# A mixture of experts on sorted rows with a register-chosen expert, in a two-layer decoder kernel

## The reference, cut to what matters

```python
xc = layernorm(x).astype(bfloat16)
normed = (xc * rsqrt(mean(xc * xc) + EPS) * norm_weight).astype(bfloat16)
logits = normed @ gate_weight.T + gate_bias            # 8 experts
scores, idx = top_k(logits, 2)
w = softmax(scores)
combine = sum(one_hot(idx, 8) * w[..., None], axis=-2)
p1 = einsum('bsh,eoh->bseo', normed, mlp1_weight) + mlp1_bias
g, lin = minimum(p1[..., 0::2], 7.0), clip(p1[..., 1::2], -7.0, 7.0)
act = g * sigmoid(1.702 * g) * (lin + 1.0)
p2 = einsum('bsei,ehi->bseh', act, mlp2_weight) + mlp2_bias
x = x + xc + einsum('bseh,bse->bsh', p2, combine).astype(bfloat16)
```

## Time and profile before

| | |
|---|---|
| median of 3 runs | 2125.4 us (2123.68 to 2129.94) |
| profiled execution | 2127.73 us, its span 2125.9 us |
| TensorE busy | 1959.0 us, 92% |
| VectorE busy | 1382.6 us, 65% |
| ScalarE busy | 1030.1 us, 48% |
| GpSimd busy | 972.0 us, 46% |
| granted TensorE clock, mean | 0.967 of full speed |
| DMA | 95.80 MB, mean 45 GB/s |
| 960 KB strips of the bias table | 16 DMAs, 6.6 us to landing (page, DMA issues) |

### The profile page before, as it was taken

How to read it: one execution, slowest core, us unless ns; L and a number is a source line. 1 busy time by engine, 2 the same in 40 slices (tenths; PEclk the granted TensorE clock), 3 DMA queues, 4 the chain that set the end, 5 groups by cost and what they waited for, 6 DMA issues and landing times.

```text
span 2125.9 us, 53677 instructions
## 1 busy us (share of the span) xinstructions
PE 1959.0 (92%) x22085; PEld 1631.0 (77%) x22085; DVE 1382.6 (65%) x3093; ACT 1030.1 (48%) x2080; POOL 972.0 (46%) x762
## 2 busy tenths in 40 slices
PE   7999999999999999857787689999999999989994
PEld 5677777777777777546676579999999999988883
DVE  6667676767676766558777675555566455456983
ACT  3666666666666665514444444333245234334551
POOL 1555555555555555524444342443433343344441
PEclk9999999999999999979999889999999999999996
DMA  7001020101010101041230120000121000030000
GB/s 256 30 18 48 19 75 18 49 21 51 16 56 11 48 11 41 13 149 40 70 110 11 50 85 8 18 12 13 48 76 52 24 25 18 17 126 26 11 16 16
DMA packets 58787, 95.80 MB, mean 45 GB/s; under 512 B 6520, under 2 KB 51328, under 8 KB 56192
## 3 DMA queue, kind: packets, MB, share of 16 engines
q1 hardware_dynamic: 55696, 84.33, 12.1%
q10 hardware_dynamic: 2848, 8.04, 1.0%
HBM read 69.93 MB, written 22.41 MB: 43 GB/s over the span
## 4 chain that ended last, share of the span: by engine, by line
PE 41%; DVE 6%; issue 4%; POOL 3%; ACT 2%; DMA 1%; SPq 0%; POOLq 0%; DVEq 0%; ACTq 0%
PE psum L262 13%; PE psum L273 9%; PE psum L1936 4%; PE psum L1924 2%; PE psum L1299 2%; PE psum L1312 2%; PE psum L1910 2%; PE psum L2428 2%; PE psum L243 2%; POOL b_act_lo L1443 1%; DVE b_act L1509 1%; PE psum L222 1%; PE psum L2462 1%; ACT e_pr L2567 1%; DMA b_wvals_in<-wvals 1%
## 5 line engine op out<-in xcount | busy, mean ns | idle before, releaser
L811 POOL TENSOR_TENSOR a_sm<-a_sm,a_rsum 128x1024 f32<-128x1024 f32 x256 | 480.2, 1895 | 384.3 <-DVE a_rsum L845 381.9
L833 DVE CUSTOM_DVE_ANT_0 a_sm<-psum,a_strip 128x1024 f32<-128x1024 f32 x256 | 312.1, 1220 | 145.7 <-PE psum L667 145.6
L748 ACT ACTIVATE a_sm<-a_sm,a_mn 128x1024 f32<-128x1024 f32 x256 | 293.9, 1148 | 27.4 <-DVE a_mn L833 26.2
L753 ACT ACTIVATE a_pT<-psum 128x512 f32<-128x512 f32 x256 | 151.6, 592 | 274.7 <-PE psum L680 274.7
L680 PE MATMUL psum<-ident,a_sm 128*128 128x128 f32 x2048 | 275.8, 277 | 5.7 <-POOL a_sm L811 4.5
L680 PEld LDWEIGHTS psum<-ident,a_sm 128*128 128x128 f32 x2048 | 224.4, 141 | 63.2 <-issue 46.3
L695 PE MATMUL psum<-a_pT,a_V 128*64 128x256 f32 x2048 | 249.0, 385 | 0.6 <-ACT a_o L759 0.6
L695 PEld LDWEIGHTS psum<-a_pT,a_V 128*64 128x64 f32 x2048 | 136.1, 136 | 77.3 <-issue 22.1
L840 DVE COPY a_pT<-psum 128x512 f32<-128x512 f32 x256 | 175.0, 684 | 13.3 <-PE psum L680 6.0
L2020 ACT ACTIVATE g_val<-psum 128x512 f32<-128x512 f32 x64 | 38.2, 598 | 216.7 <-PE psum L1936 216.7
L1443 POOL TENSOR_TENSOR b_act_lo<-b_act,b_act_hi 128x512 fp32r<-128x512 f32 x64 | 90.4, 1417 | 107.9 <-ACT b_act_hi L1350 107.9
(11 more groups left out here) (344 smaller groups left out, 4183.9 us busy)
## 6 DMA issues: line engine op xcount, KB each, us to landing
a_strip<-table SPq DMA_DIRECT2D x16, 960.0 KB, 6.6
oT<-a_o SPq DMA_DIRECT2D x64, 128.0 KB, 1.8
b_oT_in<-oT SPq DMA_DIRECT2D x8, 1024.0 KB, 5.4
a_raw<-in_a_wqkv SPq DMA_DIRECT2D x7, 384.0 KB, 3.3
s_x<-in_x_rev SPq DMA_DIRECT2D x4, 512.0 KB, 7.3
b_x_in<-in_x SPq DMA_DIRECT2D x8, 256.0 KB, 5.7
b_w<-in_m_w ACTq DMA_DIRECT2D x1, 2048.0 KB, 10.3
x<-b_x SPq DMA_DIRECT2D x8, 256.0 KB, 2.2
```

The costliest lines, as they stand in the source:

```text
L748: a.activation(sm[:, st % RING, :], sm[:, st % RING, :], ACT.Exp, scale=-1.0, bias=mn[:, at:at + 1], accum_out=rsum[:, at:at + 1]).then_in ...
L753: a.activation(probs(st, 0), psum[:, 4, :].rearrange("p (k q) -> p k q", k=4), ACT.Copy).then_inc(sig("pT_act"), 1)
L811: g.tensor_tensor(sm[:, st % RING, :], sm[:, st % RING, :], rsum[:, at:at + 1].broadcast_to([P, T]), ALU.mult).then_inc(sig("scaled"), 1)
L833: v.tensor_tensor_reduce(out=sm[:, st % RING, :], in0=scores_banks(hl).rearrange("p c n -> p (c n)"), in1=strip[:, pair % 2, hl, qt * P:qt ...
```

## The change

`cross_and_mixture` is written anew in four parts, with the same attention and expert arithmetic.

1. Rounds r = 0 to 9 instead of steps: tile r in the front of cross attention, tile r - 1 in its end and the mixture's norm, tile r - 2 in gating. Here there are no experts. Per tile the two best experts are found with max and max_index; a count of earlier rows of each expert (products of `mask` with a triangle `below` and with ones, stage `mr`) gives every row its rank. GpSimd writes each tile's normed bf16 rows with four indirect DMAs (128 rows each, for each of two experts and two tiles of 128) to `xs` in DRAM: expert e has its rows from e x 2048 on. `xs` is filled with zeros before, in self-attention, by 9 DMAs on SyncE's queue.
2. Tables: from the counts VectorE makes, for each of 23 units, its expert (`owner_i`) and first row (`first_i`); 23 = (4096 - 8) // 256 + 8 is enough for any counts. It also gathers the biases of the unit's expert, and computes for every row where its result will lie (`found_at`).
3. 23 units of 256 rows: SyncE reads the first row into a register and loads the rows, TensorE reads the expert into a register, turns the rows (`xt`, copied by ScalarE), and multiplies with w1, pick and w2 addressed by that register. The arithmetic between is that of before, with rings of 3 buffers. The bias b2 is added by two products in `down`, VectorE copies the result (`results`) and SyncE stores it to `y` in DRAM.
4. When all is stored, GpSimd gathers with four indirect DMAs per tile the two result rows of each row, and VectorE weights and adds them (`combined`). The next stage's columns, queries and keys follow all units on TensorE; its norm and key copies stand between the combinations on VectorE.

The copies of w2 and pick move from VectorE to ScalarE. Cut to its core (removed lines of the old orders are left out):

```diff
+ROUTED = E0 * N + (E0 - 1) * CP
+FILLS = -(-ROUTED // P // FILL)
...
+                    if NG // 2 <= g < NG // 2 + FILLS:
+                        i = g - NG // 2
+                        sp.wait_ge(early["have"]("fill"), 1)
+                        rows = slice(i * FILL, min((i + 1) * FILL, ROUTED // P))
+                        part = S["xs"].rearrange("(p n) d -> p n d", p=P)[:, rows, :].rearrange("p n d -> p (n d)")
+                        sp.dma_start(part, early["zeros"][:, 0:part.shape[1]]).then_inc(early["have"]("fill"), 16)
...
+        def fetch_sorted(j):
+            at_row = sp.value_load(first_i[0:1, j:j + 1], min_val=0, max_val=ROUTED - CP)
+            if j >= UR:
+                sp.wait_ge(sig("xt_ps"), j - UR + 1)
+            sp.dma_start(xs[:, j % UR, :, :], S["xs"][bass.ds(at_row, CP), :].rearrange("(t p) d -> p t d", p=P)
+                         ).then_inc(sig(f"lx{j % UR}"), 16)
...
+        sp.wait_ge(sig("tables"), 1)
+        sp.wait_ge(routed("sc"), 16 * 2 * PT * NP)
+        for j in range(UR):
+            fetch_sorted(j)
+        then["load_projections"](sp)
+        for j in range(NU):
+            if j + UR < NU:
+                fetch_sorted(j + UR)
+            store_sorted(j)
...
+    def order(r):
+        a, b, c = r, r - 1, r - 2
+        every = [("ay", a + 1), ("mT", c), ("mg", c), ("bT", a), ("bp", b), ("by", b), ("bs", a), ("mr", c), ("ay_rest", a + 1)]
+        if r == 0:
+            every = [("ay", 1), ("ay_rest", 1), ("br", 0)]
+        if r == NP + 1:
+            every.append(("mc", 0))
+        return [(stage, s) for stage, s in every if 0 <= s < NP and not (s == 0 and stage in ("bT", "bp", "bs"))]
...
+        def turned(j):
+            pe.wait_ge(sig(f"lx{j % UR}"), 16 * (j // UR + 1))
+            part_columns(pe, sig, banks, "xt", j, xs[:, j % UR, :, :], identb, dt=BF16)
...
+                        last = pe.matmul(out, w1[:, k, bass.ds(e, 1), col:col + P].rearrange("p e n -> p (e n)"), xT[:, j % UR, k, :],
+                                         start=k == 0, stop=half == 0 and k == KC - 1)
+                    if half:
+                        last = pe.matmul(out, b1r[:, :], pick[:, bass.ds(e * KC + m, 1), :].rearrange("p e n -> p (e n)"),
+                                         start=False, stop=True)
...
+                pe.matmul(out, pick[:, bass.ds(e * KC, 1), t * P:(t + 1) * P].rearrange("p e n -> p (e n)"), b2r[:, :],
+                          start=True, stop=False)
...
+                                     w2[:, bass.ds(e, 1), k, :].rearrange("p e n -> p (e n)"),
...
+        for i in every_unit:
+            if i + ahead + 1 < NU:
+                expert[i + ahead + 1] = pe.value_load(owner_i[0:1, i + ahead + 1:i + ahead + 2], min_val=0, max_val=E0 - 1)
+                turned(i + ahead + 1)
+            if 0 <= i + ahead < NU:
+                up(i + ahead)
+            if i >= 0:
+                down(i)
...
+        for n in ["columns"] + [f"q{u}" for u in range(4)] + [f"k{u}" for u in range(4)]:
+            then["first_units"](pe, n)
...
-                                    ACT.Gelu_apprx_sigmoid, bias=b1[:, e, m:m + 1])
+                last = a.activation(gs[:, j % UR, m, :], banks("ug", j)[:, m * CP:(m + 1) * CP],
+                                    ACT.Gelu_apprx_sigmoid, bias=b1s[:, m, j:j + 1])
...
+        for i in every_unit:
+            if 0 <= i + 1 < NU:
+                high(i + 1)
+            if i + ahead + 1 < NU:
+                turned(i + ahead + 1)
+            if 0 <= i + ahead < NU:
+                gated(i + ahead)
...
+        def scatter(s):
+            g.wait_ge(sig("m_spot"), s + 1)
+            g.wait_ge(have("fill"), 1 + 16 * FILLS)
+            if s:
+                g.wait_ge(routed("sc"), 16 * 2 * PT * s)
+            for slot in range(2):
+                for t in range(PT):
+                    i = slot * PT + t
+                    g.indirect_dma_start(S["xs"][:, :], bass.IndirectOffsetOnAxis(rows_at[:, s, i:i + 1], 0),
+                                         nr[:, s % 3, t, :], None).then_inc(routed("sc"), 16)
...
+        def gather(s):
+            r = s % 2
+            if s >= 2:
+                g.wait_ge(sig("m_out"), s - 1)
+            for slot in range(2):
+                for t in range(PT):
+                    i = slot * PT + t
+                    g.indirect_dma_start(yg[:, r, slot, t, :], None, S["y"][:, :],
+                                         bass.IndirectOffsetOnAxis(found_at[:, s, i:i + 1], 0)).then_inc(routed(f"gy{r}"), 16)
...
+        for r in range(1, NP + 2):
+            s, b, c = r, r - 1, r - 2
+            if s < NP:
                 norm_rstd(g, sig, "bn", s, bn, mhalf)
...
+            if 0 < b < NP:
+                g.wait_ge(sig("b_inv"), b + 1)
                 g.tensor_tensor(pr[:, :, :], pr[:, :, :], spread(mx[:, :], WK), ALU.mult).then_inc(sig("b_probs"), 1)
...
+            if c >= 1:
+                scatter(c - 1)
             if s + 1 < NP:
                 first_sum(s + 1)
-            if back:
...
+        scatter(NP - 1)
+        for j in range(NU):
+            low(j)
+        for r in range(UR):
+            g.wait_ge(sig(f"sy{r}"), 16 * len(range(r, NU, UR)))
+        g.wait_ge(sig("tables"), 2 + KC)
+        for s in range(NP):
+            gather(s)
+            if s == 3:
+                then["first_root"](g)
...
+        for r in range(1, NP + 2):
+            s, b, c = r, r - 1, r - 2
+            if 0 < b < NP:
+                shifted(b)
             if s < NP:
...
+                joined(s)
+            if c >= 0:
+                normed(c)
+            if 0 < b < NP:
+                inverse(b)
+            if s < NP:
+                v.wait_ge(sig("bT_ps"), s)
+                norm_apply(v, sig, "bn", s, x1[s % 2], h, bn)
+            if c >= 0:
+                two_best(c)
+            if b < NP:
+                crossed(b)
+            if c >= 0:
+                counted(c)
+            if b < NP:
+                squares(b)
...
+        def combined(s):
+            r = s % 2
+            v.wait_ge(routed(f"gy{r}"), 16 * 2 * PT * (s // 2 + 1))
+            if s:
+                v.wait_ge(sig("m_out"), s)
+            for t in range(PT):
+                last = v.tensor_scalar(acc[:, t, :], yg[:, r, 0, t, :], share[:, s, 0, t:t + 1], None, ALU.mult)
+            chain(last)
+            for t in range(PT):
+                last = v.scalar_tensor_tensor(accb[:, t, :], yg[:, r, 1, t, :], share[:, s, 1, t:t + 1], acc[:, t, :],
+                                              ALU.mult, ALU.add)
+            chain(last)
+            v.tensor_tensor(mo[:, :, :], xc[:, s, :, :], accb[:, :, :], ALU.add).then_inc(sig("m_out"), 1)
             v.wait_ge(sig("m_out"), s + 1)
...
+            if s >= 2:
+                v.wait_ge(sig(f"st{r}"), 16 * (1 + P // SEG) * (s // 2))
+            v.tensor_tensor(x3[:, r, :, :], x2[:, s, :, :], mo[:, :, :], ALU.add).then_inc(sig("x3"), 1)
```

More of the change, by code:

```diff
@@ L1186, in cross_and_mixture @@
-    for signals, stage, n in units:
-        turns.add(signals, [(stage, n)], range(8))
+    for r in every_round:
+        for stage, s in order(r):
+            if stage != "ay_rest":
+                turns.add(sig, [(stage, s)], range(8))
+    ahead = 2
+    every_unit = range(-ahead - 1, NU)
+    for i in every_unit:
+        if i + ahead + 1 < NU:
+            turns.add(sig, [("xt", i + ahead + 1)], range(8))
+        if 0 <= i + ahead < NU:
+            turns.add(sig, [("ug", i + ahead)], range(8))
+            turns.add(sig, [("ul", i + ahead)], range(8))
+        if i >= 0:
+            turns.add(sig, [("m2", i)], range(8))
@@ L1188, in cross_and_mixture @@
+    turns.add(following, [("dT", 0)] + [("dq", u) for u in range(4)] + [("dk", u) for u in range(4)], range(8))
     banks = turns.of(sig)
@@ new lines, in tensor, with up @@
+        for r in every_round:
+            for stage, s in order(r):
+                if stage[0] == "m" or stage == "br":
+                    routing(stage, s)
+                else:
+                    attention(stage, s)
+        expert = {}
+        def turned(j):
+            pe.wait_ge(sig(f"lx{j % UR}"), 16 * (j // UR + 1))
+            part_columns(pe, sig, banks, "xt", j, xs[:, j % UR, :, :], identb, dt=BF16)
+        def up(j):
+            e = expert[j]
+            pe.wait_ge(sig("xt_out"), j + 1)
+            for half, stage in enumerate(("ug", "ul")):
+                bank = banks.take(pe, stage, j)
@@ L1314, in down @@
             last.then_inc(sig("m2_ps"), 1)
-        for s in every_step:
-            for stage, p, n in order(s):
-                if stage == "next":
-                    then["first_units"](pe, n)
-                elif stage == "up":
-                    up(p, n)
-                elif stage == "down":
-                    down(p, n)
-                elif stage[0] == "m":
-                    gating(stage, p)
-                else:
-                    attention(stage, p)
```

(22 more changed lines are left out.)

848 lines of the change are left out of this document (377 added, 471 removed).

## The result

| | before | after |
|---|---|---|
| median | 2125.6 us (4 runs, 2123.7 to 2129.9) | 2201.7 us (4 runs, 2197.2 to 2204.3) |
| ratio | | 1.035, 95% interval 1.033 to 1.037: slower |
| profiled execution, its span | 2127.7, 2125.9 us | 2199.7, 2197.9 us |
| TensorE busy in the span | 92% | 87% |
| granted TensorE clock, mean | 0.967 | 0.93 |

The forecast was 2099 us, 26 us faster; the kernel became 76 us slower, above the range (2030 to 2165). The stage table of the kernel after shows at once which part it is. The cuts are mine: end of the first step, first turned rows of a unit, last product of a unit, first scores of the next stage. Columns are the stretch, its length, busy time (and instructions) of each engine, the granted clock, the DMA share and GB/s.

The account below looks back on a forecast made before the run. No engine full; chain gelu, product, high half, low half: 4.8 us per expert. Rounds 131.5, DRAM turn 12.0, units 107.5, then the way back put first scores at 1236.7 against 1262.7: 26 us gained, 2099 us, range 2030 to 2165.

Parts of the forecast that it names:

- Part 3: The 23 expert units: 4.3 us per unit over 25 turns, 107.5 us, to 1178.6; bounds 75 to 145 us.
- The loop that I gave as a floor: In the units, the chain gelu, product, high half, turned rows crosses two engines and back: at least 3.0 us per unit.
- The signs that the prediction named: In the new profile: indirect DMAs 1.4 us, rounds 17 us, units 4.3 us with idle before transposes, first scores at 1237.
- The sign that did fire: Prediction is wrong if time up to 902 or from the next stage's first scores on differs by over 3 us.
- Rounds: Nine rounds of cross attention and routing from attention tile 1 on: 131.5 us, to 1059.1; rounds 3 to 7 at 17 us.
- loaded earlier than they are needed: Weights wq, wk, wv of the next stage, loaded ahead of their use: counted as hidden, at nothing.
- Indirect DMAs: GpSimd's scatters in the rounds and gathers after the units: 1.42 us each, taken from its 128x512 instruction.
- Rival (a): Scatters and gathers: indirect DMAs are dear, slower from 1.9 us each; at 2.5 us each 2159 us; chance 0.16.
- Rival (c): Rounds and gathers: VectorE's steps with two SBUF inputs stop GpSimd's descriptor making, 24 us, 2123, no change; chance 0.08.
- Rival (b): Units: register reads and addressing are dear, 5.8 us per unit, 37 us more, 2136, slower; chance 0.10.
- The turn through DRAM: Between rounds and units: last scatters, landing, register read, load, transposes and copy, nothing hiding them: 12.0 us, to 1071.1.
- The tail: After the units: store, 32 gathers (45.4 us), landing, last combination (3.0), then 4.1 us to first scores at 1236.7.

## Why the prediction was wrong

**The step that failed** is Part 3, "New on TensorE's queue is one register read per unit ... 4.3 us per unit". I costed each engine's work in a unit and the loop over ScalarE and VectorE, and put the read on TensorE's queue. I never listed what is new on SyncE's queue: a store that waits for the newest result, and behind it the load for the next transposes. The diff shows both calls, one right behind the other in the same loop. The loop that I gave as a floor (gelu, product, high half, turned rows, 3.0 us) was not the longest one: copy, store, register read, load, transposes, up and down take 8.7 us. The range had 5.8 us per unit as its upper end; 8.0 came. With this order mended the unit is 3.3 us in the mean (76.1 / 23) and 3.0 in a steady turn (stores at 1136.19 and 1139.17), and the kernel takes 2089.9 us, 9 us less than the forecast. So the work was costed too high (2.9 us of TensorE's work where a turn without the read takes 2.5 to 2.6, and 1.4 us for read, restarts and addressing where 0.4 to 0.5 came), and the one waiting line at nothing. That the mended kernel lands so near 2099 us is in part luck: its units are 32 us shorter than forecast and its tail 10 longer.

The signs that the prediction named would have misled here. It expected each unit's idle time ahead of the transposes, and there it is, but TensorE waits for rows and not for a register. The sign that did fire is the last: from the first scores on, the kernel loses 3.8 to 6.4 us more, where 3 was the limit.

**Rounds** (131.5 us forecast, 5 us more measured; joins at 927.94, 939.13, 954.52, 973.59, 994.93 and 1013.77, so 11.2, 15.4, 19.1, 21.3 and 18.8 us for rounds 1 to 5 against 11, 14, 17, 17, 17). Rounds 6 to 9 made up for half of it, 50.2 us against 55.5. TensorE waited 17.0 us for row loads in four waits of the early and middle rounds, the longest behind the query weights; this accounts for 6 us of the fourth round, as the run with the late weights shows, and what the rest of the excess hangs on was not tried. TensorE was also busy less than I took, 57% of the rounds and not 74%, and its granted clock was 0.82 and not near 0.94 (945.6 to 1064.0). I had put these weights under "loaded earlier than they are needed", at nothing; moving them gave 5.4 us back. The cost of an early load lies with what stands behind it, not with what needs it.

**Indirect DMAs** (1.42 us forecast) take 0.95 us on GpSimd and 0.30 between two of them, 1.25 in all, for 128 rows of 512 or of 1024 bytes alike. From the kernel after, last scatters, a gather after its wait and the next:

```profile
1066.66 0.96 POOL L1453 DMA_INDIRECT xs<-b_nr,b_rows_at  x1 [0.31 <-issue]
1067.93 0.95 POOL L1453 DMA_INDIRECT xs<-b_nr,b_rows_at  x1 [0.30 <-issue]
1263.04 2.33 POOL L1463 DMA_INDIRECT b_yg<-y,b_found_at  x1 [5.24 <-DMA y<-b_yb]
1265.68 0.95 POOL L1463 DMA_INDIRECT b_yg<-y,b_found_at  x1 [0.31 <-issue]
```

Rival (a), indirect DMAs above 1.9 us, fell. The row that I took for it, GpSimd's own 128x512 instruction, came within 0.2 us. That is luck as much as choice: no run shows a reason why an indirect DMA should take as long as an addition.

**Rival (c)**, VectorE holding up GpSimd's descriptors, is small, and likely real. The gather of 2.33 us above began while VectorE subtracted two SBUF tiles of 128x2048, and ended 0.9 us behind it:

```profile
1262.22 2.29 DVE L2217 TENSOR_TENSOR g_wv<-g_wv_raw,g_wv 128x2048 fp32r<-128x2048 f32 x1
```

In all 13 profiles with gathers the first one stands at this place and takes 2.33 or 2.34 us, so no run parts the subtraction from being first. But GpSimd's first indirect DMA of other groups of four took 1.03 to 1.33 us, never near 2.3. Of the other 31 gathers four took 1.15 to 1.28 us, beside the combinations of tiles 0 and 2, while the one at 1303.55, beside that of tile 5, took 0.95: a combination stretches some and not others. All 32 are 33.1 us, 2.8 more than 32 at the median of 0.947. The forecast's price was 24 us. The Trainium skill ("SBUF — State Buffer", section "Who interferes with whom") says that a VectorE instruction with two SBUF inputs contends with GpSimd's reads, but that `tensor_tensor` did not stall DMAs, for which it infers as the reason that the making of descriptors needs the write side. The stretched gather beside a `tensor_tensor` speaks against that.

**Rival (b)**, the register read: TensorE's read lasts 0.302 us, with its arithmetic and assertion 0.47, SyncE's 0.272 and 0.44 (profile after, medians of 23). I had 0.9.

```profile
L1362 PEldq TENSOR_LOAD <-b_owner_i x23: 296/302/490, 1067.2 to 1241.6; - x23
L1362 PEldq FUSED_REGOPS  x23: 151/151/165, 1067.8 to 1241.9; - x23
L1200 SPq TENSOR_LOAD <-b_first_i x23: 262/272/468, 1071.5 to 1245.0; - x23
```

The floor of about 600 ns that "DMA: Bandwidth & Descriptors", section "Latency and other measured facts", of the Trainium skill states for such a load does not hold for these: both are near half of it.

**The turn through DRAM** was 10.8 us for 12.0 forecast: right.

**The tail** was 69.0 us from the last product to the first scores, 58.1 forecast (3.4, 45.4, 2.2, 3.0 and 4.1). The gathers began 3.7 us behind the last product, 0.3 later than forecast, and ran 47.8 us. 4.3 of these GpSimd waited for the statistics of the next stage's norm, work that I had set beside the gathers although it stands between them in GpSimd's queue:

```profile
1289.49 0.24 POOL L193 TENSOR_SCALAR g_dl_rs<-g_dl_mv 128x2 f32<-128x2 f32 x1 [4.28 <-DVE g_dl_mv L184]
```

Then VectorE waited 10.3 us for the first keys ahead of combinations 6 and 7 (lines of VectorE, profile after), so the combinations ended 14.8 us behind the last gather, and not 5.2 as I had it:

```profile
1315.98 0.69 DVE L2213 COPY g_kT<-psum 128x512 f32<-128x512 f32 x1 [10.27 <-PE psum L265]
1319.12 0.61 DVE L1665 TENSOR_SCALAR b_acc<-b_yg,b_share 128x256 f32<-128x256 f32 x2
1322.95 0.61 DVE L1665 TENSOR_SCALAR b_acc<-b_yg,b_share 128x256 f32<-128x256 f32 x2
```

**What was right.** The boundaries of the argument: VectorE joined tile 1 at 927.94 (927.62 before), so nothing before it changed, and the fills hid under self-attention. The number of units. That TensorE comes back to the next stage after some 35 us of idle time (33.3) and at the lower clock: 0.50 of full speed, 1.2 GHz, in the first 3 us of its query products (1301.3 to 1304.3), and 0.63 over the tail, which mixes its two levels, 1.2 and 2.4 GHz. And the forecast's gain is there to be had: it was lost to one line's place.

## What to carry to other kernels

List what a change puts on every queue, SyncE's too, and for each wait ask what stands behind it and how many iterations later its result is used: a store that waits for this iteration's result, ahead of a load for the next, makes a serial loop of a pipeline. More buffers help only where they let the load behind the wait be one for a later unit. Put stores in a load queue as many iterations late as the ring allows, or fetch that much further ahead; two units later and two more buffers gave the same time here. When one landmark is late by far, first read the chain of waits over two turns of the loop: it shows the ring in fourteen lines.

## What the runs showed of the hardware

- An indirect DMA of 128 rows on GpSimd costs 0.95 us and 0.30 us to the next, whether scatter of bf16 rows or gather of f32 rows; beside a VectorE subtraction of two SBUF tiles the first gather took 2.33 us, in every profile.
- A register read of SBUF takes 0.30 us on TensorE's queue and 0.27 on SyncE's, with some 0.17 us of arithmetic behind it. Of the 1.1 us between a store and the load behind it, 0.7 were due to this. Where TensorE is the bound, the read lengthens a turn by 0.4 us, and some turns not at all.
- With TensorE idle half of each turn its granted clock was 0.68 in the units; the same 552 products took 101.9 us of busy time there and 69.7 us at a clock of 0.95. So of the 108 us that the two-unit lag took off the units, 32 are products that ran faster, not waits that ended; a forecast that removes only the waits in the stretch (81 us) misses them.
- Executions of kernels with the same rounds began their units between 1073.4 and 1078.9 us, so a difference of 5 us between two single profiles is not a finding.
